# Edge counting in a graph network: one of four destination one-hots moves from VectorE to ScalarE

## The chip, the cores and the metric

The kernel runs on one core of a Trainium2 chip, in one launch. Its time is the device time in microseconds. Three runs of the kernel before took 3084.51, 3091.1 and 3094.24 us; their median is 3091.1 us.

## The reference

A graph of 3125 nodes (256 features each) and 100000 edges sorted by destination passes through four layers, each added to its input:

```python
x = x + L0_gnn(layernorm(x), ..., node_type_24, src, dst)   # encoder (one layer norm), then two attention layers over the edges
x = x + L0_ffn(layernorm(x)[None], ...)[0]                  # 8 experts, one chosen per node, capacity 1.25
x = x + L1_gnn(layernorm(x), src, dst, ...)                 # gated sum over the edges
x = x + L1_ffn(layernorm(x)[None], ...)[0]                  # 8 output heads, one chosen per node
```

What matters here is the encoder of `L0_gnn` and the edges. The encoder is

```python
x = concat([features, emb[input_labels]]) @ le_W1.T + le_b1
x = relu((x - mean) * rsqrt(var + 1e-5) * ln_g + ln_b)
h = x @ le_W2.T + le_b2
```

and the attention layers need, for each destination, a softmax over its incoming edges. The kernel does this densely: it first counts how many edges lead from each source to each destination, in a table `cnt`, and later multiplies by that table.

## The kernel before, in words

The program is a row of stages, each a block in which the five engines have one instruction list each and meet at semaphores. The change is in the second half of `stage_encode_count` (names beginning with `mix_` in the profile), which does two jobs at once: the encoder, over 25 blocks `b` of 128 nodes, and the counting, over 196 groups `g` of 512 edges. Eight groups (`per`) go with each block. Nothing is planned at run time: the order on each engine is written out by hand, in steps `g = 8*b + j`, j from 0 to 7.

**A group.** Its 512 edges are four columns j of 128. For each column the kernel makes a source one-hot `L[g % 4][:, j, :]` (128 edges x 128 low source digits) and a destination one-hot `R[g % 4]` (128 edges x 200, 250, 250 or 300 keys; a key is destination offset times 25 plus source block, and `SPAN` says which part of the 500 keys column j can meet). Four matmuls (`count`, L889) add up the products in a PSUM bank `p_c[g % 2]`, and VectorE adds the bank to `cnt` (`add`, L746). `L` and `R` have four buffers (`NL`), so the one-hots of group g wait for `s_cnt` of group g-4.

**Who makes them.** VectorE makes the four destination one-hots of every group, by comparing `ramp16` (uint16 key numbers) with the edge's key: `one_hots`, L738, in the order j = 3, 0, 1, 2. The source one-hots of two groups in three (g % 3 not 0, 130 groups) are made by GpSimd (L729); those of the other 66 groups by ScalarE in `near`, in two steps: four `Abs` of index minus digit into `away` (L815), then one `Relu` of 1 minus that (L819). In the 130 groups `near` returns at once.

**The encoder of a block.** TensorE: `turn_x` (transposes), `first` in two halves (L908, L909) into `p_u`, `turn_z` in two halves (L916), `second` (L924). VectorE: `moments` (L757 to L763) after `first`, `inverse` (L767, L769), `features` (L773, L774), `own_hot` (L752). ScalarE: `normalise` (L824), `copy_x` (L837, L838), `root` (L842, needs `moments`), `scaled` in two halves (L831, needs `inverse`), `affine` in two halves of four (L849, needs `turn_z`).

**The lists in order.** ScalarE, step j of block b, with g = 8b + j:

```python
if j == 0: copy_x(b + 1)
if j < 2: affine(b, j)
near(g + 3)
if j == 4: root(b + 1)
if j in (5, 6): scaled(b + 1, j - 5)
if j == 7: normalise(b + 3)
```

VectorE, the same step: `one_hots(g + 3)`, `add(g)`, and then at j = 4 `moments(b + 1)`, at 5 `inverse(b + 1)`, at 6 `features(b)`, at 7 `own_hot(b + 3)`. TensorE, block b: `turn_z(b, 0)`, count 0, `turn_z(b, 1)`, count 1, `first(b+1, 0)`, count 2, `first(b+1, 1)`, counts 3 and 4, `second(b)`, count 5, `turn_x(b+2)`, counts 6 and 7. GpSimd makes source one-hots only. SyncE stores finished rows.

Of the kernel before, what the change touches and what calls it, by code (L numbers as in the profile page):

```python
# [15 lines left out]
BF16 = mybir.dt.bfloat16  # L16
# [3 lines left out]
ACT = mybir.ActivationFunctionType  # L20
# [3 lines left out]
P = 128  # L24
N = 3125
D = 256
NB = -(-N // P)
# [4 lines left out]
ET = 4  # L32
# [28 lines left out]
CP = CG // 2  # L61
CW = 20
NL = 4
CK = NB * CW
SPAN = [(0, 8), (2, 12), (6, 16), (8, 20)]
# [342 lines left out]
def stage_encode_count(nc, C, A):  # L408

    with ExitStack() as ctx:  # L410
        sb, ps, sem = alloc(nc, ctx, "encode_")
# [7 lines left out]
        with ExitStack() as early:  # L419
            sb, ps, sem = alloc(nc, early, "prep_")  # L420
# [250 lines left out]
        sb, ps, sem = alloc(nc, ctx, "mix_")  # L671
        one = sb("one", [P, 1])
# [3 lines left out]
        ohT = [sb(f"ohlT{k}", [ST, P], BF16) for k in range(2)]  # L676
        st2 = sb("st2", [P, 2, 6]); mv2 = sb("mv2", [P, 2]); sd2 = sb("sd2", [P, 1]); rs2 = sb("rs2", [P, 1]); off2 = sb("off2", [P, 1]); off = sb("off", [P, NB])
        z = sb("z", [P, F]); zT = sb("zT", [P, FC, P]); back = sb("back", [P, P])
        L = [sb(f"L{k}", [P, ET, P], BF16) for k in range(NL)]; away = [sb(f"away{k}", [P, ET, P], BF16) for k in range(2)]
        R = [sb(f"R{k}", [P, RW], BF16) for k in range(NL)]  # L680
        p_x = ps("p_x", [P, 512]); p_u = ps("p_u", [P, 2, 512]); p_z = ps("p_z", [P, 2, 512]); p_f = ps("p_f", [P, 512])
        p_c = [ps(f"p_c{k}", [P, 512]) for k in range(2)]
        s_clear = sem("s_clear"); s_one = sem("s_one"); s_off = sem("s_off"); s_own = sem("s_own"); s_off2 = sem("s_off2")
        s_xn = sem("s_xn"); s_xT = sem("s_xT"); s_xTc = sem("s_xTc"); s_u = sem("s_u"); s_bn = sem("s_bn"); s_var2 = sem("s_var2")
        s_sd = sem("s_sd"); s_rs = sem("s_rs"); s_z = sem("s_z"); s_zT = sem("s_zT"); s_zTc = sem("s_zTc")
        s_f = sem("s_f"); s_row = sem("s_row"); s_rowd = sem("s_rowd")
        s_oh = sem("s_oh"); s_cnt = sem("s_cnt"); s_add = sem("s_add"); s_away = sem("s_away"); s_L = sem("s_L"); s_back = sem("s_back"); s_Lp = sem("s_Lp")
        feat = C.feat[:, :].rearrange("p (b h d) -> p b h d", h=H, d=HW)
        per = -(-CG // NB)
        order = [FULL] + list(range(FULL))  # L690

        def own(g, j):
            lo, hi = SPAN[j]
            at = SPAN_AT[j] + (lo * NB if j == FULL else 0)
            return R[g % NL][:, at:at + (hi - lo) * NB]

        def near_keys(j):
            return ramp16[:, SPAN[j][0] * NB:SPAN[j][1] * NB]

        def whole(g, j):  # L700
            return R[g % NL][:, SPAN_AT[j]:RW] if j == FULL else own(g, j)

        def to_count(g, j):
            lo, hi = (0, CW) if j == FULL else SPAN[j]
            return p_c[g % 2][:, lo * NB:hi * NB]

        def counted(g):
            return p_c[g % 2][:, 0:CK].rearrange("p (d b) -> p b d", b=NB)

        with nc.Block(no_gpsimd_drain=True) as block:  # L710
# [8 lines left out]
            def _(gp):  # L719
                nc.gpsimd.tensor_scalar(back[:, :], C.iota[:, :], -1.0, None, ALU.mult).then_inc(s_back, 1)  # L720
                gp.wait_ge(s_back, 1)
                for g in range(CG):
# [5 lines left out]
                    for j in range(ET):  # L728
                        nc.gpsimd.tensor_scalar(L[g % NL][:, j, :], back[:, :], lowT[:, i, j * CP + p:j * CP + p + 1], None, ALU.is_equal).then_inc(s_Lp, 1)  # L729

            @block.vector
            def _(v):
                def one_hots(g):
                    i, p = divmod(g, CP)
                    if g >= NL:
                        v.wait_ge(s_cnt, g - NL + 1)
                    for j in order:
                        nc.vector.tensor_scalar(own(g, j), near_keys(j), keyT[:, i, j * CP + p:j * CP + p + 1], None, ALU.is_equal).then_inc(s_oh, 1)  # L738

                def add(g):  # L740
                    at = v.value_load(d0i[0:1, g:g + 1], min_val=0, max_val=N - 1)
                    a = C.cnt[:, :, ds(at, CW)]
                    v.wait_ge(s_cnt, g + 1)
                    if g > 0:
                        v.wait_ge(s_add, g)
                    nc.vector.tensor_tensor(a, a, counted(g), ALU.add).then_inc(s_add, 1)  # L746

                def own_hot(b):
                    k = b % 2
                    if b >= 2:  # L750
                        v.wait_ge(s_xT, b - 1)
                    nc.vector.tensor_scalar(oh[k][:, :], iotaS[:, :], C.lab[:, b:b + 1], None, ALU.is_equal).then_inc(s_own, 1)  # L752

                def moments(b):
                    for c in range(2):
                        v.wait_ge(s_u, b * 2 + c + 1)
                        nc.vector.bn_stats(st2[:, c, :], p_u[:, c, :]).then_inc(s_bn, 1)  # L757
                    v.wait_ge(s_bn, b * 3 + 2)
                    if b >= 1:
                        v.wait_ge(s_z, b * 2)  # L760
                    nc.vector.bn_aggr(mv2[:, :], st2[:, :, :].rearrange("p a s -> p (a s)")).then_inc(s_bn, 1)
                    v.wait_ge(s_bn, b * 3 + 3)
                    nc.vector.tensor_scalar(sd2[:, :], mv2[:, 1:2], 1e-5, None, ALU.add).then_inc(s_var2, 1)  # L763

                def inverse(b):
                    v.wait_ge(s_sd, b + 1)
                    nc.vector.reciprocal(rs2[:, :], sd2[:, :]).then_inc(s_rs, 1)  # L767
                    v.wait_ge(s_rs, b + 1)
                    nc.vector.scalar_tensor_tensor(out=off2[:, :], in0=mv2[:, 0:1], scalar=-1.0, in1=rs2[:, :], op0=ALU.mult, op1=ALU.mult).then_inc(s_off2, 1)  # L769

                def features(b):
                    v.wait_ge(s_f, b + 1)
                    nc.vector.tensor_tensor(feat[:, b, :, 0:HD], p_f[:, 0:D].rearrange("p (h d) -> p h d", h=H), b21[:, 0:D].rearrange("p (h d) -> p h d", h=H), ALU.add).then_inc(s_row, 1)  # L773
                    nc.vector.tensor_tensor(C.ler[:, b * 2 * H:(b + 1) * 2 * H], p_f[:, D:D + 2 * H], b21[:, D:D + 2 * H], ALU.add).then_inc(s_row, 1)  # L774

                nc.vector.memset(one[:, :], 1.0).then_inc(s_one, 1)
                for k in range(NL):
                    nc.vector.memset(R[k][:, SPAN_AT[FULL]:RW], 0.0).then_inc(s_clear, 1)
                v.wait_ge(s_clear, NL)
                means = mv[:, :].rearrange("p (b t) -> p b t", t=2)[:, :, 0]  # L780
                nc.vector.scalar_tensor_tensor(out=off[:, :], in0=means, scalar=-1.0, in1=rstd[:, :], op0=ALU.mult, op1=ALU.mult).then_inc(s_off, 1)
                for b in range(3):
                    own_hot(b)
                for g in range(NL - 1):
                    one_hots(g)
                moments(0)
                inverse(0)
                for b in range(NB):
                    for j in range(per):
                        g = b * per + j  # L790
                        if g + NL - 1 < CG:
                            one_hots(g + NL - 1)
                        if g < CG:
                            add(g)
                        if b + 1 < NB:
                            if j == 4:
                                moments(b + 1)
                            if j == 5:
                                inverse(b + 1)
                        if j == 6:  # L800
                            features(b)
                        if j == 7 and b + 3 < NB:
                            own_hot(b + 3)

            @block.scalar
            def _(act):
                def near(g):
                    if g % 3:
                        return
                    i, p = divmod(g, CP)  # L810
                    k = g // 3 % 2
                    if g >= 6:
                        act.wait_ge(s_L, g // 3 - 1)
                    for j in range(ET):
                        nc.scalar.activation(away[k][:, j, :], C.iota[:, :], ACT.Abs, bias=lowT[:, i, j * CP + p:j * CP + p + 1]).then_inc(s_away, 1)  # L815
                    act.wait_ge(s_away, (g // 3 + 1) * ET)
                    if g >= NL:
                        act.wait_ge(s_cnt, g - NL + 1)
                    nc.scalar.activation(L[g % NL][:, :, :], away[k][:, :, :], ACT.Relu, bias=one[:, 0:1], scale=-1.0).then_inc(s_L, 1)  # L819

# [42 lines left out]
                for b in range(NB):  # L863
                    for j in range(per):
                        g = b * per + j
# [14 lines left out]
            def _(pe):  # L880
                def count(g):
                    if g >= CG:
                        return
                    pe.wait_ge(s_oh, (g + 1) * ET)
                    pe.wait_ge(s_Lp if g % 3 else s_L, (g - g // 3) * ET if g % 3 else g // 3 + 1)
                    if g >= 2:
                        pe.wait_ge(s_add, g - 1)
                    for j in order:
                        t = nc.tensor.matmul(to_count(g, j), L[g % NL][:, j, :], whole(g, j), start=(j == FULL), stop=(j == order[-1]))  # L889
                    t.then_inc(s_cnt, 1)  # L890
# [41 lines left out]
                for b in range(NB):  # L932
                    g = b * per
# [2538 lines left out]
```

## Time and profile before

| | us |
|---|---|
| median of three runs | 3091.1 |
| the profiled execution, whole | 3084.03 |
| its span (first to last instruction) | 3082.3 |
| the stage of the change, 52.4 to 436.5 | 384.1 |
| busy in the span: TensorE | 2513.6 |
| busy in the span: VectorE | 2403.9 |
| busy in the span: GpSimd | 1369.0 |
| busy in the span: ScalarE | 1169.5 |

The shares of the span are averages over stages with different limits, so the stage of the change has to be read by itself. In the rows, PE is TensorE, DVE is VectorE, ACT is ScalarE, POOL is GpSimd, and L with a number is a line of the kernel. A pair of brackets after an instruction gives the idle time just before it and what ended it.

### The profile page before, as it was taken

What the parts mean: (1) busy time and instruction counts of PE and PEld (TensorE: products, weight loads), DVE (VectorE), ACT (ScalarE), POOL (GpSimd) and SP (SyncE); (2) the same over time, 40 slices, a digit from 0 to 9 for tenths busy, and PEclk for the clock granted to TensorE, in tenths of its full rate; (3) what the DMA queues carried; (4) which work ended last, traced back from release to release, by engine and by line L of the source; (5) the groups of instructions that cost most, each with busy time, mean ns of one, the idle gap of its engine ahead of it and who ended that gap; (6) DMA issues with size and microseconds to landing.
All of it is one profiled execution on the core that took longest, in us unless ns stands there. A gap on an engine that the chain in (4) does not pass through costs nothing. (4 is left out here: it accounts for less than half of the span.)

```text
span 3082.3 us, 51388 instructions
## 1 busy us (share of the span) xinstructions
PE 2513.6 (82%) x17969; PEld 1238.1 (40%) x17970; DVE 2403.9 (78%) x5293; ACT 1169.5 (38%) x2275; POOL 1369.0 (44%) x1652
## 2 busy tenths in 40 slices
PE   6898869999987999975998766777667777677598
PEld 3555544333354333334666421333233333333365
DVE  6999979999968999988434656777777777777477
ACT  5666740000020000002221334666666666666421
POOL 2888850000000000001630877777777777775055
PEclk8999989999988999995999877888898888888799
DMA  3000010000031000013331577888888888887343
GB/s 122 10 10 10 12 36 15 15 15 15 5 48 34 15 29 15 5 44 84 100 111 48 165 221 238 250 255 251 256 257 259 255 257 259 248 259 246 125 147 105
DMA packets 235588, 373.58 MB, mean 121 GB/s; under 512 B 83274, under 2 KB 165391, under 8 KB 233514
## 3 DMA queue, kind: packets, MB, share of 16 engines
q0 software_dynamic: 75536, 238.14, 25.6%
q1 hardware_dynamic: 156569, 128.66, 14.0%
q10 hardware_dynamic: 3200, 3.21, 0.4%
q8 instruction: 153, 2.51, 0.3%
q14 instruction: 130, 1.06, 0.1%
HBM read 324.84 MB, written 50.04 MB: 122 GB/s over the span
## 5 line engine op out<-in xcount | busy, mean ns | idle before, releaser
L1091 DVE SCALAR_TENSOR_TENSOR dense_W<-layer_B,steep,cnt 128x512 f32<-128x512 f32 (+1 forms) x1400 | 834.3, 675 | 7.7 <-PE dense_p_o L1149 5.0
L1149 PE MATMUL dense_p_o<-dense_W,feat 128*32 128x512 f32 (+1 forms) x8400 | 821.3, 541 | 22.5 <-DVE dense_W L1091 22.5
L2441 POOL DMA_INDIRECT Wd<-tab_d,ixq x544 | 519.6, 955 | 169.9 <-issue 166.3
L1149 PEld LDWEIGHTS dense_p_o<-dense_W,feat 128*32 128x32 f32 x8400 | 297.0, 110 | 517.8 <-issue 396.4
L1554 POOL MEMSET edst<- 128x782 int32 x1 | 0.8, 751 | 945.9 <-POOLq L1192 945.9
L2619 PE MATMUL strips_p_sg<-strips_sv,strips_oh 128*32 128x512 f32 x2000 | 315.9, 709 | 97.5 <-DVE strips_sv L2484 97.5
L2607 PE MATMUL strips_p_b<-strips_wrs,strips_ohT 96*128 96x256 bf16 x1000 | 178.0, 308 | 220.3 <-DVE strips_ohT L2455 200.2
L729 POOL TENSOR_SCALAR mix_L<-mix_back,encode_lowT 128x128 bf16<-128x128 f32 x520 | 320.5, 634 | 55.6 <-PE mix_p_c L889 54.8
L2548 ACT ACTIVATE strips_p_s<-strips_tv 128x1024 f32<-128x1024 f32 (+1 forms) x250 | 225.2, 901 | 157.8 <-DVE strips_sv L2484 145.7
L1106 ACT COPY dense_part<-dense_p_o 128x512 f32<-128x512 f32 (+1 forms) x42 | 19.6, 540 | 669.4 <-PE dense_p_o L1149 669.4
L2441 POOL DMA_INDIRECT strips_G<-tab_d,ixq x240 | 229.5, 956 | 73.2 <-issue 71.9
L2474 DVE TENSOR_TENSOR strips_tv<-Wd,strips_p_b 128x1024 f32<-128x1024 f32 (+1 forms) x152 | 175.4, 1154 | 89.8 <-DMA Wd<-tab_d,ixq 53.0
L2607 PEld LDWEIGHTS strips_p_b<-strips_wrs,strips_ohT 96*128 96x128 bf16 x1000 | 94.0, 106 | 357.2 <-DVE strips_ohT L2455 309.7
L2551 ACT ACTIVATE strips_sv<-strips_tv 128x1024 f32<-128x1024 f32 (+1 forms) x250 | 228.6, 914 | 0.1
L2484 DVE TENSOR_TENSOR strips_sv<-Wd,strips_p_s 128x1024 f32<-128x1024 f32 (+1 forms) x152 | 174.6, 1149 | 67.9 <-ACT strips_p_s L2548 67.8
L738 DVE TENSOR_SCALAR mix_R<-encode_ramp,encode_keyT 128x250 bf16<-128x250 uint16 (+2 forms) x784 | 183.2, 299 | 0.0
L746 DVE TENSOR_TENSOR cnt<-cnt,mix_p_c 128x500 f32 x196 | 130.7, 667 | 23.8 <-PE mix_p_c L889 21.4
L889 PE MATMUL mix_p_c<-mix_R,mix_L 128*128 128x250 bf16 (+2 forms) x784 | 128.6, 291 | 14.9 <-DVE cnt L746 12.6
L2630 PE MATMUL strips_p_sg<-strips_nil 128*128 128x512 bf16 x400 | 137.6, 479 | 0.0
L2652 PEld LDWEIGHTS strips_p_h<-strips_xT,strips_w 128*128 128x128 f32 x768 | 103.6, 214 | 65.9 <-issue 65.9
L2619 PEld LDWEIGHTS strips_p_sg<-strips_sv,strips_oh 128*32 128x32 f32 x2000 | 42.1, 115 | 194.8 <-DVE strips_sv L2484 142.4
L2652 PE MATMUL strips_p_h<-strips_xT,strips_w 128*128 128x128 f32 x768 | 117.1, 307 | 0.0
(530 smaller groups left out, 3816.6 us busy)
## 6 DMA issues: line engine op xcount, KB each, us to landing
strips_row<-dlr_d SPq DMA_DIRECT2D x250, 96.0 KB
ew<-in_ew SPq DMA_DIRECT2D x16, 1024.0 KB, 5.4
layer_B<-rise_d SPq DMA_DIRECT2D x12, 1024.0 KB
hx_d<-strips_hrow SPq DMA_DIRECT2D x24, 512.0 KB
Wd<-tab_d,ixq POOLq DMA_INDIRECT x544
Wd<-in_fWd SPq DMA_DIRECT2D x8, 1024.0 KB, 8.6
tab_d<-feat SPq DMA_DIRECT2D x50, 128.0 KB, 2.5
tab_d<-gated_in_rowg SPq DMA_DIRECT2D x25, 256.0 KB, 2.0
```

What stands on the lines that cost most here:

```text
L729: nc.gpsimd.tensor_scalar(L[g % NL][:, j, :], back[:, :], lowT[:, i, j * CP + p:j * CP + p + 1], None, ALU.is_equal).then_inc(s_Lp, 1)
L738: nc.vector.tensor_scalar(own(g, j), near_keys(j), keyT[:, i, j * CP + p:j * CP + p + 1], None, ALU.is_equal).then_inc(s_oh, 1)
L1091: o = nc.vector.scalar_tensor_tensor(out=out, in0=rise, scalar=C.steep[:, q * H + h:q * H + h + 1], in1=count, op0=ALU.max, op1=ALU.mult)
L1149: m = nc.tensor.matmul(p_o[c % 2][h * MT:(h + 1) * MT, a, 0:n], feat[:, q, h, lo:lo + MT], W[t % 3][:, h, 0:n], start=(q == 0), stop=(q == ...
L2441: gp.indirect_dma_start(out=G[n % RING][:, j, :], out_offset=None, in_=C.tab3[:, :], in_offset=bass.IndirectOffsetOnAxis(ap=index, axis=0) ...
L2474: nc.vector.tensor_tensor(tv[g % 2][:, 0:wide(g), :], rows(g)[:, :, 0:D], p_b[:, 0:wide(g), :], ALU.add).then_inc(s_t, 1)
L2484: nc.vector.tensor_tensor(sv[g % 2][:, 0:wide(g), 0:D], rows(g)[:, :, D:2 * D], p_s[:, 0:wide(g), :], ALU.mult).then_inc(s_use, 1)
L2548: nc.scalar.activation(p_s[:, 0:wide(g), :], tv[g % 2][:, 0:wide(g), :], ACT.Sigmoid).then_inc(s_s2, 1)
L2551: nc.scalar.activation(sv[g % 2][:, 0:wide(g), D:2 * D], tv[g % 2][:, 0:wide(g), :], ACT.Sigmoid).then_inc(s_s, 1)
L2607: t = nc.tensor.matmul(p_b[:, j % wide(g), :], ohT[g % 2][:, j * P:j * P + P], wrs[b % 3][:, j, :], start=(j < wide(g)), stop=(wide(g) == ...
L2619: t = nc.tensor.matmul(p_sg[b % 2][j * QP:(j + 1) * QP, :], oh[g % 4][:, j, :], sv[g % 2][:, j % wide(g), :], start=(i == 0), stop=(i == Q ...
L2652: t = nc.tensor.matmul(ffn(b)[:, q * P:q * P + P], w1[:, kc, q * P:q * P + P], xT[:, kc * P:kc * P + P], start=(kc == 0), stop=(kc == KC - 1))
```

## The change

In the 130 groups whose source one-hots GpSimd makes, ScalarE makes destination one-hot 0 (the 200-key one) in two steps, into a new two-buffer tile `far` and from there into `R`; VectorE makes the other three. TensorE's `count` waits for one more semaphore, `s_oa`. ScalarE's `near(g)` keeps its place in the list.

```diff
+ far = [sb(f"far{k}", [P, (SPAN[0][1] - SPAN[0][0]) * NB], BF16) for k in range(2)]
...
-                    for j in order:
+                    for j in order if g % 3 == 0 else order[:1] + order[2:]:
                         nc.vector.tensor_scalar(own(g, j), near_keys(j), keyT[...], None, ALU.is_equal).then_inc(s_oh, 1)
...
+                def near_hot(g):
+                    n = g - g // 3 - 1
+                    i, p = divmod(g, CP)
+                    if n >= 2:
+                        act.wait_ge(s_oa, n - 1)
+                    nc.scalar.activation(far[n % 2][:, :], near_keys(0), ACT.Abs, scale=-1.0, bias=keyT[:, i, p:p + 1]).then_inc(s_far, 1)
+                    act.wait_ge(s_far, n + 1)
+                    if g >= NL:
+                        act.wait_ge(s_cnt, g - NL + 1)
+                    nc.scalar.activation(own(g, 0), far[n % 2][:, :], ACT.Relu, bias=one[:, 0:1], scale=-1.0).then_inc(s_oa, 1)
+
                 def near(g):
                     if g % 3:
+                        near_hot(g)
                         return
...
-                    pe.wait_ge(s_oh, (g + 1) * ET)
+                    pe.wait_ge(s_oh, (g + 1) * ET - (g - g // 3))
+                    if g:
+                        pe.wait_ge(s_oa, g - g // 3)
```

## Rows read from the trace of the kernel before

**Rows 1.** Busy time by engine in the stage and in three blocks; columns: stretch, length, engines.
```profile
52.40:436.50 384.10, 340.52 (x1709) 214.73 (x1709) 348.38 (x1211) 257.54 (x680) 321.02 (x521) 0.98 0.04 10
202.56:247.56 45.00, 40.49 (x209) 25.68 (x207) 42.21 (x149) 31.01 (x84) 39.45 (x65) 1.00 0.04 10
```

**Rows 2.** Waits of ScalarE in these blocks: total, times, longest.
```profile
ACT mix_sd L842 <- DVE mix_sd L763: 10.6, 3, 4.5
ACT mix_z L831 <- DVE mix_off L769: 3.1, 2, 1.6
```

**Rows 3.** Groups of ScalarE instructions, 100 to 400 us: count, busy, mean ns, idle before.
```profile
L815 ACT ACTIVATE mix_away<-iota,encode_lowT 128x128 bf16<-128x128 f32 x212 | 67.7, 402 | 0.0
...
L819 ACT ACTIVATE mix_L<-mix_away,mix_one 128x512 bf16<-128x512 bf16 x53 | 38.2, 722 | 1.7
```

**Rows 4.** The 200-key one-hots among VectorE's instructions of the three blocks.
```profile
L738 DVE TENSOR_SCALAR mix_R<-encode_ramp,encode_keyT 128x200 bf16<-128x200 uint16 x24 | 6.2, 258 | 0.0
```

**Rows 5.** ScalarE in order of time over the three blocks: start, duration, instruction, count.
```profile
201.13 1.43 ACT L831 ACTIVATE mix_z<-mix_p_u,mix_off,mix_rs 128x512 f32<-128x512 f32 x2
...
204.74 1.29 ACT L815 ACTIVATE mix_away<-iota,encode_lowT 128x128 bf16<-128x128 f32 x4
206.06 0.72 ACT L819 ACTIVATE mix_L<-mix_away,mix_one 128x512 bf16<-128x512 bf16 x1
206.69 1.49 ACT L849 ACTIVATE mix_zT<-mix_p_z,encode_bcol,encode_gcol 128x128 f32<-128x128 f32 x4
...
215.43 0.78 ACT L831 ACTIVATE mix_z<-mix_p_u,mix_off,mix_rs 128x512 f32<-128x512 f32 x1 [1.55 <-DVE mix_off L769]
216.10 1.27 ACT L815 ACTIVATE mix_away<-iota,encode_lowT 128x128 bf16<-128x128 f32 x4
...
218.03 0.76 ACT L831 ACTIVATE mix_z<-mix_p_u,mix_off,mix_rs 128x512 f32<-128x512 f32 x1
...
230.62 1.45 ACT L831 ACTIVATE mix_z<-mix_p_u,mix_off,mix_rs 128x512 f32<-128x512 f32 x2 [1.56 <-DVE mix_off L769]
...
233.88 0.59 ACT L824 ACTIVATE mix_xn<-X,mix_off,encode_rstd 128x256 f32<-128x256 f32 x1
...
234.63 0.26 ACT L838 CAST mix_ohlT<-mix_p_x 96x128 bf16<-96x128 f32 x1
...
237.54 1.29 ACT L815 ACTIVATE mix_away<-iota,encode_lowT 128x128 bf16<-128x128 f32 x4
...
244.10 0.20 ACT L842 ACTIVATE mix_sd<-mix_sd 128x1 f32<-128x1 f32 x1 [4.51 <-DVE mix_sd L763]
...
246.13 1.43 ACT L831 ACTIVATE mix_z<-mix_p_u,mix_off,mix_rs 128x512 f32<-128x512 f32 x2
```

**Rows 6.** TensorE's matmuls in order of time, 203 to 236 us.
```profile
208.99 1.19 PE L889 MATMUL mix_p_c<-mix_R,mix_L 128*128 128x500 bf16 x8
210.01 3.73 PE L924 MATMUL mix_p_f<-encode_w,mix_zT 128*128 128x264 f32 x16
...
219.85 1.89 PE L908 MATMUL mix_p_u<-encode_w,mix_xT 128*128 128x512 f32 x4
...
224.25 1.19 PE L889 MATMUL mix_p_c<-mix_R,mix_L 128*128 128x500 bf16 x8
225.27 3.73 PE L924 MATMUL mix_p_f<-encode_w,mix_zT 128*128 128x264 f32 x16
...
234.94 1.55 PE L908 MATMUL mix_p_u<-encode_w,mix_xT 128*128 128x512 f32 x3 [0.37 <-ACT mix_ohlT L838]
```

**Rows 7.** VectorE in order of time, 203 to 232 us.
```profile
204.06 0.94 DVE L738 TENSOR_SCALAR mix_R<-encode_ramp,encode_keyT 128x300 bf16<-128x300 uint16 x4
204.88 0.66 DVE L746 TENSOR_TENSOR cnt<-cnt,mix_p_c 128x500 f32 x1
...
228.66 0.15 DVE L763 TENSOR_SCALAR mix_sd<-mix_mv 128x1 f32<-128x1 f32 x1
...
230.42 0.16 DVE L769 SCALAR_TENSOR_TENSOR mix_off<-mix_mv,mix_rs 128x1 f32<-128x1 f32 x1
```

More of the change, by code:

```diff
@@ L678, in stage_encode_count @@
         z = sb("z", [P, F]); zT = sb("zT", [P, FC, P]); back = sb("back", [P, P])
-        L = [sb(f"L{k}", [P, ET, P], BF16) for k in range(NL)]; away = [sb(f"away{k}", [P, ET, P], BF16) for k in range(2)]
+        L = [sb(f"L{k}", [P, ET, P], BF16) for k in range(NL)]; away = [sb(f"away{k}", [P, ET, P], BF16) for k in range(2)]; far = [sb(f"far{k}", [P, (SPAN[0][1] - SPAN[0][0]) * NB], BF16) for k in range(2)]
         R = [sb(f"R{k}", [P, RW], BF16) for k in range(NL)]
@@ L682, in stage_encode_count @@
         p_c = [ps(f"p_c{k}", [P, 512]) for k in range(2)]
-        s_clear = sem("s_clear"); s_one = sem("s_one"); s_off = sem("s_off"); s_own = sem("s_own"); s_off2 = sem("s_off2")
+        s_clear = sem("s_clear"); s_far = sem("s_far"); s_oa = sem("s_oa"); s_one = sem("s_one"); s_off = sem("s_off"); s_own = sem("s_own"); s_off2 = sem("s_off2")
         s_xn = sem("s_xn"); s_xT = sem("s_xT"); s_xTc = sem("s_xTc"); s_u = sem("s_u"); s_bn = sem("s_bn"); s_var2 = sem("s_var2")
```

## The prediction

> **What bounds the kernel now.** I read the busy time of the stage first: VectorE is busy 348.4 of 384.1 us, TensorE 340.5, GpSimd 321.0, ScalarE 257.5 [rows 1]. Over three blocks in the middle, where the pattern of groups repeats (24 groups are three blocks and eight times "every third"), 45.00 us pass: VectorE 42.21, TensorE 40.49, GpSimd 39.45, ScalarE 31.01, at a granted clock of 1.00, which is the higher level, 2.4 GHz [rows 1]. VectorE looks like the bound and ScalarE like the engine with 14 us to spare.
>
> The waits say what this spare time is. Of it, 10.6 us go before `root` and 3.1 us before `scaled` [rows 2]: ScalarE has run ahead with its one-hots and then stands in order behind one result of VectorE. So the next view is time order, where a round is visible. I take a round from the end of the second half of `scaled` (time S) to the same point one block later. S falls at 202.56, 218.79, 232.07 and 247.56 [rows 5], so the rounds last 16.23, 13.28 and 15.49 us, 45.00 in all, and differ by where ScalarE's source one-hots fall:
>
> - round Y (from 202.56): the ScalarE group is 8b+3, and again 8b+6 and 8b+9;
> - round Z (from 218.79): 8b+4 and 8b+7;
> - round X (from 232.07): 8b+2, 8b+5 and 8b+8.
>
> A round is a loop through all three engines: S, `copy_x`, the two halves of `first`, counts 8b+3 and 8b+4, `second`, count 8b+5, its `add`, `inverse`, the two halves of `scaled`. Beside it runs a branch over `moments` and `root`. In Z this loop has almost no slack: `first` starts 1.06 after S, the pair of counts at 5.46, `second` at 6.48 [rows 6], `inverse` ends at 11.79 (230.42 + 0.16) [rows 7], and the two halves of `scaled` run at once, from 11.83 to 13.28 [rows 5]. In X, `first` already waits 0.37 us for `copy_x` [rows 6], because a source one-hot stands ahead of it on ScalarE.
>
> **What the change removes.** 130 one-hots of 200 keys on VectorE. A record is 258 ns [rows 4], but neighbours overlap: four one-hots of 1000 keys together take 0.82 us from the first's start to the next `add` (204.06 to 204.88) [rows 7], so 200 keys are worth 0.16 (all by key) to 0.205 (a quarter); I take 0.18. That is 0.93 us a block and 23.4 us in all, if VectorE sets the pace.
>
> **What it adds: the price of a group on ScalarE.** No row shows an `Abs` on uint16 or a 200-wide `Relu`. The nearest are the same two functions, with a bias by partition, at 128 (402 ns) and 512 (722 ns) [rows 3]: on the line between them 200 columns take 0.46 us. The `Relu` has to wait for its `Abs`; in the same pattern this costs 0.03 (206.03 to 206.06), and the next instruction overlaps the `Relu` by 0.09 (206.78 against 206.69) [rows 5]. So a group costs 0.46 + 0.03 + 0.37 = 0.86 us. Bounds for it: at the lower end both steps as cheap as the shortest row, 0.20 for one column (`root`) [rows 5], 0.33 with the same gaps; at the upper end both at 0.72 as if 512 wide, 1.38. I take 0.86, since the line runs through the same functions on both sides of 200.
>
> By load alone, 16 groups x 0.86 = 13.8 us fill the 14.0 us that ScalarE has spare in three blocks. But this work isn't put into the spare time: it is in a fixed order ahead of `copy_x`, ahead of the one-hots that TensorE waits for, and between the halves of `scaled`.
>
> The Trainium skill ("ScalarE: Activation LUTs", section "Rules for kernel authors") tells one to give `relu` and its like to VectorE and not to ScalarE. The rows here agree for this operation, 0.18 us against 0.86. The same page ("What ACT_TABLE_LOAD costs") gives 280 ns + 0.833 ns a column with such a bias, 447 ns for 200, and 93 ns of overlap; by these the group is 0.83 and the sum below 26 us in place of 27.
>
> **The sum, round by round.** A source one-hot of ScalarE takes 1.95 us (204.74 to 206.69), `normalise`, `copy_x` and both `affine` together 3.66 (233.88 to 237.54), the part to the end of `copy_x` 1.01 [rows 5]. The first of a round's groups starts 0.1 before S.
>
> *Z.* `copy_x` now ends at -0.1 + 0.86 + 1.01 = 1.77 after S, and `first` starts 0.05 later (234.89 to 234.94 in X [rows 5, 6]), at 1.82 and not 1.06. The counts come 4.40 later (219.85 to 224.25) [rows 6], the second of the pair 0.51 after the first, at 6.73. But that one needs the one-hot of 8b+4, ScalarE's own, which is ready at -0.1 + 0.86 + 3.66 + 0.86 + 1.95 + 0.09 = 7.32. So it starts at 7.35, `second` at 7.86 and no longer 6.48, and all behind it shifts by 1.38: `inverse` ends at 13.17. Is `root` in time? ScalarE reaches it at -0.1 + 2 x 1.95 + 4 x 0.86 + 3.66 = 10.9; `moments` ends at 10.02 + 1.38 = 11.40 (228.66 + 0.15 shifted) [rows 7]; with 0.24 for `root` and 0.86 for 8b+8 it is 12.5, before 13.17. Then `scaled`, the new group between its halves, `scaled`: 13.21 + 0.67 (215.43 to 216.10) + 0.86 + 0.76 = 15.50. Before: 13.28. Loss 2.22.
>
> *Y.* The same sums up to `second`, at 7.86 (the source one-hot is now in 8b+3). Before, it was at 7.45 (210.01) [rows 6], because VectorE was late, so VectorE's gain shows here, and is used up: `inverse` at 13.17, then 0.67 + 1.93 + 0.76 with the source one-hot between the halves, as before: 16.57. Before: 16.23. Loss 0.34.
>
> *X.* The source one-hot already stood ahead of `copy_x`, so `first` and the counts don't move: 8b+4 is ready at 7.32, the pair began at 2.87 + 4.40 = 7.27 and its second count at 7.78. ScalarE is at `root` at 10.9, ahead of the 12.03 of before (244.10, after a wait of 4.51) [rows 5]. Only the new group between the halves is added: 0.67 + 0.86 + 0.76 in place of 1.43. Loss 0.86.
>
> Together 3.42 us in three blocks, 48.4 for 45.0. There are 24 rounds, eight such triples: 27.4 us. Two of the 130 groups are made before the first round, where ScalarE waits for `moments` of block 0; I cost them at nothing, at most 1.7 us. After the last round no group is left. At the price of 0.33 the same sums give 0.33 (X), 0.63 (Z) and -0.72 (Y): 0.24, or 2 us in all. At 1.38 ScalarE reaches `root` only at 12.98, and they give 2.33, 4.13 and 1.73: 8.2, or 66 us. GpSimd's waits are untouched, and it gets more time.
>
> The profiled execution took 3084.0 us, 7.1 below the median of the runs, 3091.1. With 27.4 it is 3111; on the median it is 3118. I put the forecast between, at 3115.
>
> **The rivals.**
>
> *VectorE sets the pace and ScalarE's work is hidden.* One place, L738 on VectorE: it loses 0.18 us in 130 groups and everything follows it. For it: VectorE is busy 42.21 of 45.00 [rows 1]. Against: in Z and X the loop goes through TensorE and ScalarE. It decides only if a group costs ScalarE clearly less than 0.33, where Y's gain outweighs X and Z. Time: 3088 - 23 = 3065.
>
> *Hidden and worth nothing.* The 13.8 us fall into ScalarE's 13.7 us of waits [rows 2], and `copy_x` and the halves of `scaled` turn out not to be in the loop. For it: the two numbers match. Against: the 0.37 us that `first` waits in X, and the 1.55 before `scaled` [rows 5, 6], which show that both are. Time: 3084 to 3094.
>
> *ScalarE becomes the bound altogether*, its new steps dearer than the line (a type that no row shows, or a wait between the steps above 0.03). Time: up to 3088 + 66 = 3154, ScalarE without a wait before `root`.
>
> **How the numbers follow.** I give the forecast 0.62, the dear ScalarE 0.14, hidden 0.14, VectorE's pace 0.10. A measurement of this kernel can tell about 0.3%, 9 us. Slower by more than this is the forecast and the dear case, 0.76; no change 0.14; faster 0.10. The likeliest case by itself, with a group between 0.75 and 1.0 us and either base, is 3103 to 3126. The range for 8 in 10 takes in half of the hidden case below and the greater part of the dear case above: 3088 to 3142.
>
> **What the profile after would show.** Blocks of 16.1 us and not 15.0, the stage some 411 us long; 130 `Abs` of about 0.46 us and as many `Relu`; ScalarE's waits before `root` down from 10.6 to 2 to 3 us in three blocks; VectorE with three one-hots in two groups of three and longer waits for TensorE's counts; TensorE waiting for `copy_x` in all rounds and for ScalarE's one-hots at count 8b+4. If the blocks stay at 15.0 us, `copy_x` and `scaled` weren't in the loop. If a group takes well under 0.5 us, the price was wrong. If blocks fall to 14, VectorE was the bound. If TensorE's granted clock falls in the stage, the sum does not hold at all.

## The result and the profile after

The changed kernel took 3116.26 us (median of five runs, 3111.71 to 3119.11), the kernel before 3084.51 us in the same comparison (five runs, 3082.04 to 3094.24): 31.7 us more between the medians. The ratio, which goes by all the runs, is 1.0093 with a 95% interval of 1.0073 to 1.0114, or 28.7 us. The forecast was 3115 us and 27 us slower.

| us | before | after |
|---|---|---|
| profiled execution | 3084.03 | 3117.32 |
| its span | 3082.3 | 3115.6 |
| first S to last S (24 rounds) | 360.7 | 389.1 |
| start of `features` of the last block | 435.94 | 465.02 |

The stage ends 29.1 us later; the remaining 4.2 us of the span lie in stages whose instructions are the same in both. The rounds alone make 28.4 us. Each kind has the same length all along the stage, to 0.04 us, but for the first and the last round and two stretched ones (last section).

The busy time over three rounds, X, Y and Z, of the changed kernel; the columns are those of [rows 1].

```profile
192.89:241.38 48.49, 41.70 (x207) 25.42 (x207) 39.73 (x133) 43.83 (x115) 38.87 (x65) 1.00 0.04 10
```

The 45.00 us of [rows 1] have become 48.49, with TensorE's granted clock at 1.00, the higher level, in both. VectorE's busy time fell from 42.21 to 39.73 and ScalarE's rose from 31.01 to 43.83. No engine is busy all the time: ScalarE, the busiest, still has 4.7 us without work. The waits of ScalarE in this stretch answer to [rows 2]:

```profile
ACT mix_z L843 <- DVE mix_off L769: 3.0, 2, 1.6
ACT mix_sd L854 <- DVE mix_sd L763: 0.9, 1, 0.9
```

The wait before `root` is nearly gone (10.6 to 0.9), the one before `scaled` is as it was. TensorE's waits in the same stretch show what came instead:

```profile
...
PE mix_p_u L922 <- ACT mix_ohlT L850: 2.2, 3, 1.2
PE mix_p_c L903 <- ACT mix_L L831: 0.6, 1, 0.6
```

`first` (L922) now waits for `copy_x` in all three rounds, where it waited in one, and in Z count 8b+4 waits for ScalarE's own source one-hot. The new steps, grouped by line between 100 and 400 us:

```profile
L816 ACT ACTIVATE mix_R<-mix_far,mix_one 128x200 bf16<-128x200 bf16 x100 | 46.2, 462 | 3.2
L812 ACT ACTIVATE mix_far<-encode_ramp,encode_keyT 128x200 bf16<-128x200 uint16 x100 | 45.2, 452 | 0.0
```

ScalarE in order of time, to be read against [rows 5]:

```profile
204.73 0.20 ACT L854 ACTIVATE mix_sd<-mix_sd 128x1 f32<-128x1 f32 x1 [0.91 <-DVE mix_sd L763]
...
207.42 0.45 ACT L812 ACTIVATE mix_far<-encode_ramp,encode_keyT 128x200 bf16<-128x200 uint16 x1
207.90 0.46 ACT L816 ACTIVATE mix_R<-mix_far,mix_one 128x200 bf16<-128x200 bf16 x1
208.27 0.76 ACT L843 ACTIVATE mix_z<-mix_p_u,mix_off,mix_rs 128x512 f32<-128x512 f32 x1
208.93 0.45 ACT L812 ACTIVATE mix_far<-encode_ramp,encode_keyT 128x200 bf16<-128x200 uint16 x1
209.41 0.46 ACT L816 ACTIVATE mix_R<-mix_far,mix_one 128x200 bf16<-128x200 bf16 x1
209.78 0.59 ACT L836 ACTIVATE mix_xn<-X,mix_off,encode_rstd 128x256 f32<-128x256 f32 x1
...
222.29 0.78 ACT L843 ACTIVATE mix_z<-mix_p_u,mix_off,mix_rs 128x512 f32<-128x512 f32 x1 [1.39 <-DVE mix_off L769]
...
224.89 0.76 ACT L843 ACTIVATE mix_z<-mix_p_u,mix_off,mix_rs 128x512 f32<-128x512 f32 x1
...
232.23 0.72 ACT L831 ACTIVATE mix_L<-mix_away,mix_one 128x512 bf16<-128x512 bf16 x1
...
239.09 0.78 ACT L843 ACTIVATE mix_z<-mix_p_u,mix_off,mix_rs 128x512 f32<-128x512 f32 x1 [1.57 <-DVE mix_off L769]
...
240.62 0.76 ACT L843 ACTIVATE mix_z<-mix_p_u,mix_off,mix_rs 128x512 f32<-128x512 f32 x1
```

A group takes 0.85 us from its `Abs` to the next instruction (208.93 to 209.78). One stands between the halves of `scaled` (207.42), one ahead of `normalise` and `copy_x` (208.93). S is at 209.03, 225.65 and 241.38. TensorE in round Z of this kernel, to be read against [rows 6]:

```profile
227.46 1.98 PE L922 MATMUL mix_p_u<-encode_w,mix_xT 128*128 128x512 f32 x4 [0.58 <-ACT mix_ohlT L850]
...
231.95 0.68 PE L903 MATMUL mix_p_c<-mix_R,mix_L 128*128 128x500 bf16 x4
233.24 0.67 PE L903 MATMUL mix_p_c<-mix_R,mix_L 128*128 128x500 bf16 x4 [0.61 <-ACT mix_L L831]
233.75 3.73 PE L938 MATMUL mix_p_f<-encode_w,mix_zT 128*128 128x264 f32 x16
```

`first` is at S + 1.81, `second` at S + 8.10; in [rows 6] they were at 1.06 and 6.48. The pair of counts has come apart: the second of it waits for the one-hot that ScalarE ends at 232.95. In Y it comes apart too, there over the new destination one-hot of 8b+4; ScalarE, then TensorE:

```profile
215.88 0.46 ACT L816 ACTIVATE mix_R<-mix_far,mix_one 128x200 bf16<-128x200 bf16 x1
```

```profile
216.44 0.67 PE L903 MATMUL mix_p_c<-mix_R,mix_L 128*128 128x500 bf16 x4 [0.43 <-issue]
216.95 3.73 PE L938 MATMUL mix_p_f<-encode_w,mix_zT 128*128 128x264 f32 x16
```

The profile names no releaser for this wait (`issue`), but the `Relu` ends at 216.34, 0.10 us before it is over. `second` is at S + 7.92.

### The profile page after: what moved, and what is told of

Same layout as the page of the kernel before. It is cut to its first block and busy times, and to the rows that moved or that the text cites. A ratio compares the mean times of both kernels' runs of the same rounds, so it can differ in the third digit from the quotient of the medians.

```text
span 3115.6 us, 51840 instructions
## 1 busy us (share of the span) xinstructions
PE 2529.3 (81%) x17969; PEld 1232.8 (40%) x17970; DVE 2383.7 (77%) x5163; ACT 1274.1 (41%) x2535; POOL 1365.7 (44%) x1652
## 5 line engine op out<-in xcount | busy, mean ns | idle before, releaser
L1163 PEld LDWEIGHTS dense_p_o<-dense_W,feat 128*32 128x32 f32 x8400 | 290.1, 110 | 524.5 <-issue 399.1
L738 DVE TENSOR_SCALAR mix_R<-encode_ramp,encode_keyT 128x250 bf16<-128x250 uint16 (+2 forms) x654 | 158.7, 304 | 0.0
```

The source lines that it names most:

```text
L1163: m = nc.tensor.matmul(p_o[c % 2][h * MT:(h + 1) * MT, a, 0:n], feat[:, q, h, lo:lo + MT], W[t % 3][:, h, 0:n], start=(q == 0), stop=(q == ...
```

## The experiments

Each kernel is compared with the kernel before on the same chip. The first four after the changed one ran on one chip and the last four on another, so across these groups the ratios are compared and not the medians. A diff is against the changed kernel where nothing else is said, and shows the main lines. Theory: a step on ScalarE costs by its **place** in the fixed order of the round. Rivals: it costs by ScalarE's **load**; or VectorE sets the **pace**, and its relief counts. The table gives the median length of a round of each kind, measured in the trace from S to S (the kinds go by block, b mod 3 = 0, 1, 2), and the ratio to the kernel before with its interval.

| kernel | Y | Z | X | three blocks | ratio |
|---|---|---|---|---|---|
| before | 16.23 | 13.27 | 15.50 | 45.00 | |
| changed | 16.62 | 15.71 | 16.14 | 48.47 | 1.0093 (1.0073 to 1.0114) |
| relief_only | 16.17 | 13.27 | 15.28 | 44.72 | 0.9988 (0.9978 to 0.9997) |
| steps_only | 16.09 | 15.54 | 16.35 | 47.98 | 1.0074 (1.0058 to 1.0089) |
| one_step | 15.83 | 14.21 | 15.63 | 45.67 | 1.0025 (1.0017 to 1.0034) |
| reordered | 14.61 | 15.68 | 15.12 | 45.41 | 1.0010 (0.9999 to 1.0021) |
| partial_567 | 16.37 | 13.27 | 15.29 | 44.93 | 1.0006 (0.9995 to 1.0016) |
| partial_234 | 16.61 | 14.89 | 15.50 | 47.00 | 1.0061 (1.0043 to 1.0079) |
| before_reordered | 14.34 | 15.16 | 14.88 | 44.38 | 0.9978 (0.9966 to 0.9989) |
| reordered_567 | 14.44 | 15.31 | 14.68 | 44.43 | 0.9982 (0.9972 to 0.9992) |

**VectorE's relief alone** (relief_only).

```diff
                     if g % 3:
-                        near_hot(g)
                         return
...
-                    if g:
-                        pe.wait_ge(s_oa, g - g // 3)
```

> VectorE makes three one-hots in the 130 groups, and nobody makes the fourth (its columns keep what an earlier group left there), so this times VectorE's relief by itself. Theory (the round's loop sets the pace): only the round in which VectorE was late (Y) gains, 0.6 to 0.9 us, X about 0.2 and Z nothing: 7 to 9 us under the kernel before, about 3076 us. Rival (VectorE sets the pace): the full 130 x 0.18 = 23 us, about 3061 us. Rival (nothing hangs on it): within 3 us of before.

It took 3081.4 us against 3084.5: 3.7 us less by the ratio (0.9 to 6.8). The rival of the pace falls, since 23 us were to come. The theory's 7 to 9 us did not come either: X gained its 0.2, but Y only 0.06, and the time is close to that of the other rival, by which nothing hangs on the relief. VectorE at the start of a Y round, in the kernel before:

```profile
200.68 0.90 DVE L738 TENSOR_SCALAR mix_R<-encode_ramp,encode_keyT 128x300 bf16<-128x300 uint16 x4
201.50 0.66 DVE L746 TENSOR_TENSOR cnt<-cnt,mix_p_c 128x500 f32 x1
...
202.50 0.86 DVE L738 TENSOR_SCALAR mix_R<-encode_ramp,encode_keyT 128x300 bf16<-128x300 uint16 x4
203.27 0.66 DVE L746 TENSOR_TENSOR cnt<-cnt,mix_p_c 128x500 f32 x1
```

VectorE and then TensorE at the same place in relief_only:

```profile
200.91 0.68 DVE L738 TENSOR_SCALAR mix_R<-encode_ramp,encode_keyT 128x300 bf16<-128x300 uint16 x3
201.64 0.68 DVE L746 TENSOR_TENSOR cnt<-cnt,mix_p_c 128x500 f32 x1
202.23 0.42 DVE L773 TENSOR_TENSOR feat<-mix_p_f,encode_b 128x256 f32<-128x256 f32 x1
...
202.64 0.75 DVE L738 TENSOR_SCALAR mix_R<-encode_ramp,encode_keyT 128x300 bf16<-128x300 uint16 x3
203.31 0.66 DVE L746 TENSOR_TENSOR cnt<-cnt,mix_p_c 128x500 f32 x1
```

```profile
204.12 0.67 PE L901 MATMUL mix_p_c<-mix_R,mix_L 128*128 128x500 bf16 x4 [0.54 <-DVE cnt L746]
```

Count 8b+1 waits for the `add` of 8b-1, at the end of a chain on VectorE that starts with count 8b-3: `add`, `inverse`, one-hots, `add`, `features`, one-hots, `add`. It holds only two groups of one-hots. Both are relieved, and they take 0.73 and 0.67 us to the next `add` in place of 0.82 and 0.77: 0.1 less each, and not 0.18. That is used up, because X ends 0.2 us sooner: count 8b-3 starts 3.33 us before S and not 3.54 (199.25, and 199.02 in the kernel before), and count 8b+1 comes 1.54 after S where it came 1.52 after.

**ScalarE's steps alone** (steps_only).

```diff
-                    for j in order if g % 3 == 0 else order[:1] + order[2:]:
+                    for j in order:
...
-                    nc.scalar.activation(own(g, 0), far[n % 2][:, :], ...)
+                    nc.scalar.activation(aside[n % 2][:, :], far[n % 2][:, :], ...)
...
-                    pe.wait_ge(s_oh, (g + 1) * ET - (g - g // 3))
-                    if g:
-                        pe.wait_ge(s_oa, g - g // 3)
+                    pe.wait_ge(s_oh, (g + 1) * ET)
```

> ScalarE makes both new steps, but into a tile that nobody reads, and VectorE still makes all four one-hots; TensorE doesn't wait for ScalarE's. This times ScalarE's steps without the relief. Theory: the steps cost by their place in ScalarE's order, so rounds of about 16.7, 15.7 and 16.3, 3113 to 3122 us, within 6 us of the changed kernel. Rival (VectorE's relief is worth its full 23 us): 3116 + 23, about 3139 us. Rival (TensorE's wait for the new one-hots is the cost, not the steps): 3084 to 3092 us.

It took 3107.87 us, 23 us over before and below the expected range; that is 6 us under the changed kernel by the ratios (8 between the medians), with intervals that overlap, and the rounds in the traces differ in the same direction. So the steps by themselves make 2.98 of the 3.47 us in three blocks, though no instruction outside ScalarE reads their result. The halves of `scaled` that end its rounds:

```profile
209.90 0.76 ACT L843 ACTIVATE mix_z<-mix_p_u,mix_off,mix_rs 128x512 f32<-128x512 f32 x1
...
225.98 0.76 ACT L843 ACTIVATE mix_z<-mix_p_u,mix_off,mix_rs 128x512 f32<-128x512 f32 x1
...
241.53 0.76 ACT L843 ACTIVATE mix_z<-mix_p_u,mix_off,mix_rs 128x512 f32<-128x512 f32 x1
...
257.88 0.76 ACT L843 ACTIVATE mix_z<-mix_p_u,mix_off,mix_rs 128x512 f32<-128x512 f32 x1
```

They lie 16.08, 15.55 and 16.35 us apart; 16.7, 15.7 and 16.3 were expected, so Y is the miss. Against it the changed kernel has the relief (X is 0.21 shorter) and one thing more, TensorE's wait for the new one-hots: Y is 0.53 longer and Z 0.17. In Y, count 8b+4 is a group of GpSimd's, so without that wait ScalarE does not hold it up: `second` starts 7.32 after S (210.66) and not 7.92.

```profile
217.98 3.73 PE L936 MATMUL mix_p_f<-encode_w,mix_zT 128*128 128x264 f32 x16
```

**Half the price** (one_step). The `Relu` is left out, the `Abs` goes to a tile that no matmul reads, and TensorE waits for it.

> Only the Abs is made, into a tile that no matmul reads, and TensorE waits for it; the Relu is left out, so the fourth one-hot of the 130 groups is not made. A group costs ScalarE about 0.36 us in place of 0.85. Theory (price times place): by the sums of the three rounds Y -0.4, Z +1.0, X +0.2 us, 6 us in all, 3086 to 3094 us. Rival (ScalarE's load alone decides: 31 + 16 x 0.36 = 37 us of 45 fit into its idle time): the gain of the relief alone, 3061 to 3078 us.

3092.45 us, 7.7 us over before by the ratio, with Z +0.94, X +0.13 and Y -0.40, as the sums had it. A group's price is read between the halves of `scaled` of its Z round, which start 1.03 us apart and not 0.67 [rows 5]:

```profile
231.81 0.78 ACT L842 ACTIVATE mix_z<-mix_p_u,mix_off,mix_rs 128x512 f32<-128x512 f32 x1 [1.44 <-DVE mix_off L769]
232.49 0.45 ACT L815 ACTIVATE mix_far<-encode_ramp,encode_keyT 128x200 bf16<-128x200 uint16 x1
232.84 0.77 ACT L842 ACTIVATE mix_z<-mix_p_u,mix_off,mix_rs 128x512 f32<-128x512 f32 x1
```

With 0.35 us a group (232.49 to 232.84) ScalarE is far from full, and it still costs: here load does not explain it.

**The same work in another order** (reordered).

```diff
                         g = b * per + j
-                        if j == 0 and b + 1 < NB:
-                            copy_x(b + 1)
-                        if j < 2:
-                            affine(b, j)
+                        if j == 0 and b == 0:
+                            copy_x(b + 1)
+                        if j == 0:
+                            affine(b, j)
                         if g + NL - 1 < CG:
                             near(g + NL - 1)
+                        if j == 1:
+                            affine(b, j)
+                            if b + 3 < NB:
+                                normalise(b + 3)
                         if j == 4 and b + 1 < NB:
                             root(b + 1)
-                        if j in (5, 6) and b + 1 < NB:
-                            scaled(b + 1, j - 5)
-                        if j == 7 and b + 3 < NB:
-                            normalise(b + 3)
+                        if j == 5 and b + 1 < NB:
+                            scaled(b + 1, 0)
+                            scaled(b + 1, 1)
+                            if b + 2 < NB:
+                                copy_x(b + 2)
```

> The changed kernel with the same instructions on ScalarE in another order: both halves of scaled together, copy_x of the next block right behind them, the second affine behind the one-hots of 8b+4, normalise behind that. Theory (place): second can start about 1 us sooner after scaled, and rounds fall from 16.16 to about 15.0 to 15.3 us, where ScalarE's own work of 44.8 us in three blocks ends it: 3088 to 3098 us. Rival (ScalarE is full, and the order is of no matter): 3116 us as it is.

3087.68 us: not one instruction less than in the changed kernel, and about 26 us less time by the ratios (28.6 between the medians). Here ScalarE is nearly full, as its busy time between 100 and 400 us shows (fourth of the engines), and of its waits only the one for `inverse` is left:

```profile
100.00:400.00 300.00, 268.38 (x1371) 169.96 (x1369) 262.08 (x868) 288.87 (x755) 255.27 (x424) 1.00 0.05 10
```

```profile
ACT mix_z L843 <- DVE mix_off L769: 6.0, 13, 0.5
```

That its load sets the time in this order is argued from these rows; no run here takes the load away and keeps the places.

**As many groups in two places** (partial_567 and partial_234). Both give ScalarE the steps of 48 or 49 of the 130 groups; the others stay with VectorE.

```diff
+        hots = [g for g in range(CG) if g % 3 and g % 8 in (5, 6, 7)]    # or (2, 3, 4)
...
-                        near_hot(g)
+                        if g in hots:
+                            near_hot(g)
```

> The change in only 6 of 16 of its groups, those of 8b+5 to 8b+7, whose steps fall into ScalarE's wait before root. Theory (place): nothing is lost, and VectorE's relief gives about what it gave alone in X: 0.1 to 0.3 us in three blocks, 3080 to 3085 us. Rival (load, cost in proportion to the groups): 31.7 x 6/16 = 12 us more than before, about 3096 us.

> The change in as many groups, 6 of 16, but in those of 8b+2 to 8b+4, whose steps stand ahead of copy_x and of the one-hots that count 8b+4 needs. Theory (place): Z +1.6 us (second at about 8.1 after S in place of 6.48), Y +0.45, X nothing: 2.0 us in three blocks, 16 us in all, 3098 to 3103 us. Rival (load): the same as with 8b+5 to 8b+7, about 3096 us if the cost goes by groups.

3086.39 us, where no difference from before can be told (X is 0.21 us shorter and Y 0.14 longer), and 3103.64 us, 18.8 us over it by the ratio. Both lie just above the expected ranges. The number of steps is the same, to one group; only the place differs. TensorE's `second` and the two halves of `scaled` around a Z round of partial_234:

```profile
231.08 3.73 PE L941 MATMUL mix_p_f<-encode_w,mix_zT 128*128 128x264 f32 x16
```

```profile
222.27 0.76 ACT L846 ACTIVATE mix_z<-mix_p_u,mix_off,mix_rs 128x512 f32<-128x512 f32 x1
...
236.42 1.45 ACT L846 ACTIVATE mix_z<-mix_p_u,mix_off,mix_rs 128x512 f32<-128x512 f32 x2 [2.38 <-DVE mix_off L771]
```

With S at 223.03, `second` is at 8.05 and was expected at 8.1. In the first three of its Z rounds the length was 15.8 us and later 14.8. The reason is TensorE's granted clock, which fell in each of these three and not in the later ones (the number after the busy times; third and fourth Z round):

```profile
175.12:190.93 15.81, 14.75 (x65) 8.72 (x65) 11.86 (x41) 10.74 (x29) 11.05 (x20) 0.89 0.01 2
223.03:237.87 14.84, 13.21 (x65) 8.17 (x65) 11.77 (x41) 10.73 (x29) 11.11 (x20) 1.00 0.01 2
```

Without it Z is 14.84, and the three rounds make about 3 of the 377 us from the first S to the last.

**The order without the change, and with a part of it** (before_reordered and reordered_567). The diff of reordered on the kernel before, and on partial_567.

> The kernel before, with ScalarE's list in the other order (both halves of scaled together, copy_x behind them, the second affine behind the one-hots of 8b+4). Theory (the loop over ScalarE's order sets the pace, not VectorE's load of 14.07 us a block): Y loses the source one-hot between its halves and X the one ahead of copy_x; blocks of 14.1 to 14.5 us, 12 to 22 us under before, 3063 to 3073 us. Rival (VectorE's load with its waits is the bound): 3080 to 3088 us.

> The other order on ScalarE, and the change in the groups of 8b+5 to 8b+7 only. Theory: what the order gives and a little relief where VectorE is then nearer to the bound: 3058 to 3072 us, the fastest. If VectorE's relief is worth nothing even there, the time of the reordered kernel before; if ScalarE's load counts as such, above it.

3076.01 and 3077.37 us: both beat the kernel before (ratios 0.9978 and 0.9982) and the changed one, and can't be told from each other: 48 groups moved neither gain nor cost anything here. The whole change in this order (reordered) is about 10 us slower than the order alone by the ratios (1.0010 and 0.9978). Both times lie above the expected ranges: the order gained 6.8 us by the ratio, where 12 to 22 were to come. Two of TensorE's waits in before_reordered, 100 to 400 us:

```profile
PE mix_p_c L894 <- DVE cnt L746: 9.1, 19, 0.7
...
PE mix_p_c L894 <- ACT mix_L L819: 6.1, 5, 1.2
```

The wait for VectorE's `add` in the kernel before, in the same stretch:

```profile
PE mix_p_c L889 <- DVE cnt L746: 9.0, 20, 0.7
```

It is as large in both. New is the wait for ScalarE's source one-hots (L894, five times, 6.1 us). It falls in Z, where the one-hot of 8b+1 now comes behind both halves of `scaled` and `copy_x`; here S is at 212.29:

```profile
214.74 0.67 PE L894 MATMUL mix_p_c<-mix_R,mix_L 128*128 128x500 bf16 x4 [1.21 <-ACT mix_L L819]
```

`first` stands right behind this count on TensorE and starts 2.96 after S in place of 1.06. So Z loses in this order the 1.89 us that Y gains, which the expectation did not foresee: again a matter of place.

## Why the prediction was right

The place in ScalarE's order decides, as forecast: the steps of as many groups cost nothing that can be told in one place and 19 us in another (partial_567, partial_234), the steps without the relief make most of the loss (steps_only), and with all of them in another order the kernel is back at the time of before (reordered). By the ratios the change costs 29 us in the old order and about 10 us in the new one. Whether these 10 us are ScalarE's load or again a matter of place, no run separates; the forecast did not separate it either.

That the time came out 1.3 us from the forecast is partly luck. The forecast stood on a base of 3088 us, and the kernel before took 3084.51 in the comparison; the 3.5 us too much made up for time that I had put at nothing. In the sum, Z was 0.21 us too short and X 0.21 too long.

| | forecast | measured |
|---|---|---|
| price of a group | 0.86 us | 0.85 |
| Y | 16.57 | 16.62 |
| Z | 15.50 | 15.71 |
| X | 16.35 | 16.14 |
| eight times the three | +27.4 | +27.8 |
| 24 rounds, first and last and stretched ones as they were | | +28.4 |

Point by point:

- **The price.** The line between 128 and 512 columns gave 0.46 us for each step; they took 0.45 and 0.46, and uint16 at the input was no dearer. By an estimate from the figures of the Trainium skill ("ScalarE: Activation LUTs", section "What ACT_TABLE_LOAD costs") a step is 447 ns; the trace has means of 452 and 462.
- **Z.** `first` at 1.81 (forecast 1.82), the one-hot of 8b+4 ready at 7.30 (7.32). Count 8b+4 started 0.29 us after that and not 0.03, and this is what Z had too little, 0.23 in the round shown (15.73).
- **Y.** `second` at 7.92 (7.86), but the reason beside it was wrong. I wrote that Y was long because VectorE was late and that its gain is used up there. The relief alone gave Y 0.06 us: Y begins with a chain of `add`s on which only two of the relieved groups lie, and what holds `second` at 7.92 is ScalarE's destination one-hot of 8b+4, as steps_only shows (7.32, and Y 16.09, without TensorE's wait for it).
- **X.** Only the group between the halves of `scaled` was to be added. It was, but the relief, which I had put at nothing here, brings `root` forward: it starts at S + 11.84 (204.73) and not at 12.03 [rows 5], and X is 0.21 us shorter than forecast.
- **VectorE's pace**, the rival on the other side, falls: 23 us were its price, and relief_only gave 3.7 us. VectorE was busy for 94% of the time, and yet with 130 of its instructions gone the rounds got only 0.28 us shorter in three blocks.
- **Hidden** falls, though the match of 13.8 and 13.7 us was real: ScalarE's wait before `root` did shrink, to 0.9 us where I had said 2 to 3, but other steps stood ahead of what TensorE waits for. **The dear ScalarE** falls by the price.
- **Outside the rounds** I put nothing. In the traces the first S came 1.6 us earlier, the end after the last S took 2.3 us more, and the later stages 4.2 us more. Of the 2.3 us the last `second` makes 1.7 (5.52 us long and not 3.83): TensorE's granted clock was 0.85 from the last S to `features`, and 1.00 in the kernel before. The rest is left open, since the runs of one kernel differ by up to 12 us.
- **Two slips** in the working change nothing: with 0.20 us for both steps the lower price is 0.34 and not 0.33, and a group of 0.75 us on the lower base gives 3106 and not 3103.

## What to carry to other kernels

Idle time of an in-order engine is not room. Find the loop that ends a period, mark which instructions of the engine lie on it, and ask of added work what it stands ahead of; 0.85 us ahead of a copy that TensorE waits for put TensorE's matmul back by 0.75 us (in Z, from 1.06 to 1.81 after S), on an engine that idled a third of the time. And an engine that is busy for 94% may still not be the pace: take its work away in an experiment (leave it out) before paying for moving it. If the trace gives a loop that sums to the period before, its sums can serve for the period after: here they met each kind of round to 0.21 us. They miss where a branch that they leave out ends last, as VectorE's chain did in relief_only and ScalarE's one-hot of 8b+1 in before_reordered.

## What else the runs showed

Single rounds are stretched with no change of work. In the changed kernel one Z round is 16.65 us long in place of 15.71 and one X round 17.83 in place of 16.14, and the first half of `first` in this X round takes 3.50 us and not 1.98:

```profile
244.26 3.50 PE L922 MATMUL mix_p_u<-encode_w,mix_xT 128*128 128x512 f32 x4 [1.20 <-ACT mix_ohlT L850]
```

TensorE's granted clock fell there, between two stretches at 1.00 (the number after the busy times). From 245 to 247 us it is 0.50, the lower level, 1.2 GHz:

```profile
200.00:240.00 40.00, 34.96 (x180) 22.11 (x179) 32.66 (x108) 35.47 (x93) 31.99 (x53) 1.00 0.03 7
240.00:252.00 12.00, 10.25 (x41) 5.02 (x42) 7.89 (x27) 11.77 (x32) 8.58 (x16) 0.86 0.06 13
245.00:247.00 2.00, 2.00 (x4) 0.81 (x3) 0.68 (x4) 1.97 (x6) 0.46 (x1) 0.50 0.04 8
252.00:300.00 48.00, 41.24 (x207) 25.02 (x206) 39.34 (x131) 41.77 (x110) 38.51 (x64) 1.00 0.04 9
```

TensorE had waited 1.20 us just before; but all X rounds of this kernel wait there, seven of them for about 1.20 us, and seven of eight kept the clock. The stretched Z round has a mean of 0.90. The kernel before has one such round as well (Z, 14.94 in place of 13.27, granted clock 0.89). What makes the clock fall stays open.

TensorE's start after a wait has a price that the waits of before did not show at this place: 0.29 us from the end of ScalarE's source one-hot (232.95) to the matmul (233.24) that it held up last. After the destination one-hot in Y it was 0.10 us (216.34 to 216.44). Why the two differ isn't shown.
